# Rows of second chunks scaled between the halves of the value copy, first chunks' squares behind the next row copy, and a wait of its own for third chunks' last tile

## What is computed

```python
e = stack([tbl_f[ids[:, f]] for f in range(26)], axis=1)          # 512 x 26 x 64
x = layer_norm(dense @ Wd.T, gd, bd)                              # 512 x 128
y = layer_norm(einsum('bnd,ed->bne', e, Ws), gs, bs)              # 512 x 26 x 128
y = layer_norm(einsum('bne,pn->bep', y, Wsi), gsi, bsi)           # 512 x 128 x 32
T = concatenate([x[:, None, :], swapaxes(y, 1, 2)], axis=1)       # 512 x 33 x 128
Z = einsum('bnd,bmd->bnm', T, T)                                  # pair products
z = layer_norm(Z[:, TRIL_I, TRIL_J] @ Wl.T, gl, bl) * mask        # 512 x 512, 384 live
h = relu(concat([z, dense]) @ W_top1 + b1); h = relu(h @ W_top2 + b2)
out = h @ W_top3                                                  # 512 x 1
```

## Time and profile before

| what | us |
|---|---|
| median of three runs | 169.57 |
| time of the profiled execution | 170.27 |
| its span, first to last instruction | 168.4 |
| around the span | 1.87 |
| TensorE, VectorE, ScalarE, GpSimd busy | 147.9, 125.5, 82.7, 100.7 |

### The profile page before, as it was taken

The page is one execution under the profiler, slowest core; times in us unless marked ns, Lnnn a source line. Parts: engine busy times, 40 slices in busy tenths (PEclk is TensorE's granted clock), DMA queues, the critical chain, the costliest instruction groups (busy, mean ns, idle before and its releaser), DMA issues.

```text
span 168.4 us, 3523 instructions
## 1 busy us (share of the span) xinstructions
PE 147.9 (88%) x1378; PEld 106.1 (63%) x1378; DVE 125.5 (74%) x258; ACT 82.7 (49%) x226; POOL 100.7 (60%) x109
## 2 busy tenths in 40 slices
PE   0298978989799589999999899999998999889995
PEld 0133446957456457557978465778876665679983
...
DMA packets 5728, 8.14 MB, mean 48 GB/s; under 512 B 2357, under 2 KB 3279, under 8 KB 5712
## 3 DMA queue, kind: packets, MB, share of 16 engines
...
...
## 4 chain that ended last, share of the span: by engine, by line
POOL 49%; issue 24%; PE 17%; DMA 3%; ACT 2%; POOLq 1%; DVE 1%; SPq 1%; DVEq 0%
POOL G L333 49%; DMA smask<-in_span_mask_dram 3%; PE ps_y L1003 2%; PE ps_tail L1034 2%; PE ps_ut L1218 2%; PE ps_y L1202 1%; PE ps_tail L1161 1%; PE ps_z L1007 1%; POOLq L95 1%; PE ps_z L1034 1%; PE ps_z L1181 1%; PE ps_y L1092 1%; PE ps_gq L1060 1%; PE ps_z L1202 1%; PE ps_gq L1202 1%
## 5 line engine op out<-in xcount | busy, mean ns | idle before, releaser
L333 POOL DMA_INDIRECT G<-in_table_dram,idx x104 | 98.6, 948 | 34.6 <-issue 31.1
L1072 PE MATMUL ps_ut<-S,G 128*128 128x192 f32 (+4 forms) x128 | 21.9, 316 | 2.3 <-DVE G L775 2.3
L1072 PEld LDWEIGHTS ps_ut<-S,G 128*128 128x128 f32 x128 | 20.1, 199 | 4.0 <-DVE G L775 2.6
L789 DVE TENSOR_TENSOR V<-ps_y,bias_y 128x512 f32<-128x512 f32 x32 | 20.5, 683 | 1.3 <-PE ps_y L1085 1.2
L1092 PEld LDWEIGHTS ps_z<-V 128*64 128x64 f32 x448 | 14.3, 136 | 11.3 <-DVE V L805 6.5
L796 DVE TENSOR_REDUCE var<-sq 128x32 f32<-128x1024 f32 x14 | 17.1, 1221 | 5.6 <-ACT sq L439 5.6
L439 ACT ACTIVATE sq<-V 128x1024 f32<-128x1024 f32 x14 | 14.9, 1063 | 11.7 <-DVE V L789 11.5
L1085 PE MATMUL ps_y<-ut,wcg 64*128 64x512 f32 x64 | 18.1, 639 | 2.6 <-issue 1.5
L1092 PE MATMUL ps_z<-V 128*64 128x67 f32 x448 | 16.2, 224 | 0.8 <-DVE V L805 0.7
L1060 PE MATMUL ps_gq<-gram,gt 128*128 128x128 f32 x104 | 15.5, 289 | 1.6 <-ACT gt L425 1.4
L1060 PEld LDWEIGHTS ps_gq<-gram,gt 128*128 128x128 f32 x104 | 13.3, 198 | 2.8 <-ACT gt L425 1.7
...
## 6 DMA issues: line engine op xcount, KB each, us to landing
G<-in_table_dram,idx POOLq DMA_INDIRECT x104, 2.5
...
```

Source lines behind the costliest of these rows:

```text
L333: pool.indirect_dma_start(G[:, n // NC, j, g, :], None, table, bass.IndirectOffsetOnAxis(ap=idx[:, k:k + 1], axis=0)).then_inc(gathered[n ...
L789: dve.tensor_tensor(chunk_v(n)[:, g * CB // 2:(g + 1) * CB // 2, :, :], ps_y[:, g, :].rearrange("p (b l q) -> p b l q", l=2, q=NPROJ), bia ...
L1072: mm = pe.matmul(ps_ut[:, chunk % 2, col:col + width], G[:, gp, j, :, :].rearrange("p g d -> p (g d)"), S[:, j, :, :].rearrange("p s q -> ...
```

## The change

On VectorE, in slots c = 1 the rows of chunk n are scaled between the two halves of the value copy of chunk n - 1, and `variance2` of the first chunk leaves that slot; it stands in slot c = 2 after the two copies of `x_slots` and in front of `normalise2` (not in slot 2, where the chunk's variance is taken before the slots begin). On ScalarE, `square2` of the first chunk leaves slot c = 1 and stands in slot c = 2 behind `gt_copy`, with `ut_copy` behind it and `deviation2` after that; `relu2` goes in front of `deviation1`. On TensorE, the transposes of a third chunk begin after two tiles have arrived and wait for the third on a semaphore of its own; SyncE's load of the second part of wl waits for two tiles of chunk 2 instead of three. No instruction on data is added or removed.

```diff
--- before.py
+++ after.py
@@ -192,6 +192,7 @@
         ld_ids, ld_wc, ld_ws, ld_wd, ld_pm, ld_sm, ld_s, ld_x, ld_w1z, ld_w1d, ld_w2, ld_gs = [
             sem(n) for n in ("ld_ids", "ld_wc", "ld_ws", "ld_wd", "ld_pm", "ld_sm", "ld_s", "ld_x", "ld_w1z", "ld_w1d", "ld_w2", "ld_gs")]
         ld_wl = [sem("ld_wl_a"), sem("ld_wl_b")]
+        last_tile_gathered = [sem(f"last_tile_gathered{gp}") for gp in range(NG)]
         gathered = [[sem(f"gathered{gp}_{c}") for c in range(NC)] for gp in range(NG)]
 
         (idx_ready, consts_set, wc_ready, wcg_ready, wc_nat_ps, wc_nat_sb, gram_ps, gram_ready, patterns_ready, wsis_ready,
@@ -302,7 +303,7 @@
             sp.dma_start(pmask[:, :], pair_mask).then_inc(ld_pm, 16)
             sp.dma_start(mmask[:, :], merge_mask).then_inc(ld_pm, 16)
             for h, (k, end) in enumerate(((0, 2), (2, KB))):
-                sp.wait_ge(gathered[0][1 + h], 2 * len(batch(1 + h)) * 16)
+                sp.wait_ge(gathered[0][1 + h], 2 * (len(batch(1 + h)) - h) * 16)
                 sp.dma_start(wl[:, k:end, :], wl_blocks[:, k:end, :]).then_inc(ld_wl[h], 16)
             sp.wait_ge(gathered[0][3], 2 * len(batch(3)) * 16)
             sp.dma_start(w2s[:, :, :], w2).then_inc(ld_w2, 16)
@@ -332,7 +333,8 @@
                                 pool.wait_ge(done, value)
                         pool.indirect_dma_start(
                             G[:, n // NC, j, g, :], None, table,
-                            bass.IndirectOffsetOnAxis(ap=idx[:, k:k + 1], axis=0)).then_inc(gathered[n // NC][n % NC], 16)
+                            bass.IndirectOffsetOnAxis(ap=idx[:, k:k + 1], axis=0)).then_inc(
+                                last_tile_gathered[n // NC] if n % NC == 2 and j == js[-1] else gathered[n // NC][n % NC], 16)
 
             n = NCHUNK - 2
             pool.wait_ge(r2_ready, n + 1)
@@ -549,11 +551,15 @@
                     deviation3(gp - 1)
                 if not early:
                     gt_copy(n)
-                if c < 3:
+                if c < 2:
                     deviation2(n - 2)
+                if c == 2:
+                    square2(n - 2)
                 if c == 3 and gp > 0:
                     f_scale(gp - 1)
                 ut_copy(n - 1)
+                if c == 2:
+                    deviation2(n - 2)
                 if c == 0 and gp > 1:
                     relu1(gp - 2)
                 if c == 2 and gp > 0:
@@ -567,13 +573,14 @@
                 if n == 6:
                     prepare_gains((4,))
                     dense_direct(2)
-                deviation1(n)
                 if c == 1 and gp > 1:
                     relu2(gp - 2)
+                deviation1(n)
                 if c == 3 and gp > 0:
                     zn_copy(gp - 1)
-                square2(n - 1)
-                if c == 1:
+                if c != 1:
+                    square2(n - 1)
+                else:
                     z_evacuate(n - 2)
                 if c == 1 and gp > 1:
                     y_copy(gp - 2)
@@ -783,8 +790,8 @@
                     dve.tensor_copy(V[:, :, 1:3].rearrange("p (c i h) l -> p c i h l", h=2, c=NC)[:, :, :, h, :],
                                     x_sb[:, gp * GRAN:(gp + 1) * GRAN].rearrange("p (h l c i) -> p c i h l", h=2, l=2, c=NC)[:, :, :, h, :])
 
-            def y_evacuate(n):
-                for g in range(2):
+            def y_evacuate(n, halves=(0, 1)):
+                for g in halves:
                     dve.wait_ge(y_ps, 2 * n + 1 + g)
                     dve.tensor_tensor(chunk_v(n)[:, g * CB // 2:(g + 1) * CB // 2, :, :],
                                       ps_y[:, g, :].rearrange("p (b l q) -> p b l q", l=2, q=NPROJ),
@@ -917,17 +924,20 @@
                     z_merge(n - 3)
                 if c == 2 and gp > 0:
                     x_slots(gp)
+                    variance2(n - 2)
                 normalise2(n - 2)
                 if c == 3 and gp > 0:
                     root3(gp - 1)
                 if c == 0 and gp > 1:
                     add_dense(gp - 2)
                 variance1(n)
-                y_evacuate(n - 1)
+                y_evacuate(n - 1, (0, 1) if c != 1 else (0,))
                 scale_rows(n)
-                variance2(n - 1)
                 if c == 1:
+                    y_evacuate(n - 1, (1,))
                     z_merge(n - 2)
+                else:
+                    variance2(n - 1)
                 if n == 3:
                     prepare_shift()
 
@@ -1046,11 +1056,14 @@
 
             def transpose_rows(n):
                 gp, j, count = rows_of(n)
-                pe.wait_ge(gathered[gp][n % NC], 2 * count * 16)
+                split = n % NC == 2
+                pe.wait_ge(gathered[gp][n % NC], 2 * (count - split) * 16)
                 if n > 0:
 
                     pe.wait_ge(q_used, n)
                 for i in range(count):
+                    if split and i == count - 1:
+                        pe.wait_ge(last_tile_gathered[gp], 2 * 16)
                     mm = pe.transpose(ps_gq[:, i * P:(i + 1) * P], G[:, gp, j + i, :, :].rearrange("p g d -> p (g d)"), eye[:, :])
                 mm.then_inc(gt_ps, 1)
```

## The result

The changed kernel takes 173.79 us (median of 6 runs, 172.28 to 174.49), the kernel before 170.16 (median of 6 beside them, 169.30 to 171.87). The ratio is 1.0228, with a 95% interval of 1.0198 to 1.0259: slower, by a little more than 2% as far as the interval can tell. The prediction was 172.4 us, range 170.6 to 173.8, with 0.70 on a difference within 2% and 0.28 on slower by more. So the time lies just inside the range and the sign was right, but 3.6 us came where the sum gave 2.85, and the case on which most of the chance lay did not come.

What follows compares the result with a forecast made beforehand. TensorE's embed waiting for VectorE's first-chunk norm chain was taken as the bound, gathers a floor beneath. Delays of 1.45 + 0.70 + 0.70 = 2.85 us on 169.57 gave 172.4 us, range 170.6 to 173.8.

Steps and rivals of the forecast that it cites:

- the sum: Delays of embed in slots 6, 10 and 14 add 1.45 + 0.70 + 0.70 = 2.85 us to the time.
- the case on which most of the chance lay: Whole kernel: time differs by less than 2% (3.4 us) from the kernel before; chance 0.70.
- What bounds the kernel: Slots 6, 10, 14: embed starts 0.10 us after the first chunk's product, sharing its bank; gathers are a floor TensorE touches.
- The squares behind the row copy: Slots 6, 10, 14: squares to embed runs in series, 4.46 us; slot 6's embed comes 1.45 us later.
- The value copy's second half: Slots 10 and 14: split copy ends 2.09 us after its start instead of 1.28; embed 0.70 us later each.
- What these delays do afterwards: TensorE after embed: each delay is kept until the next slot c = 2 and reaches the end in full.
- What is saved: Earlier relu2 (0.74 us), VectorE's variance wait (0.43) and earlier row scaling (0.5) are counted at nothing.
- the lower end of 2.1: If the row copy held the squares, savings count: total 1.45 at slot 6, about 1.75 at 10, 2.1 us at 14.
- The gathers' own waits: GpSimd: gather 51 starts at 67.94, 0.2 us late, later ones lose some 0.3 more; hidden behind TensorE's lag.
- The last tile's own wait: Third chunks' transposes: separate wait worth zero, between -0.3 and +0.05 us; the earlier wl load also zero at the end.
- TensorE's clock falls in the new gaps: Rival, slots 6, 10, 14: lower clock costs 1.7 us three times, 5.1 in all, giving 177.5 us; chance 0.04.
- The rule that I set against the trace: Trainium skill on TensorE: waits inside a loop drop the clock again each time; would give the clock rival's 177.5 us.

Runs made afterwards that it cites:

- experiment 2: Changed kernel with first chunks' second-norm reciprocals in an SBUF tile and no wait of embed for the product: 172.09 us, ratio 1.0154.
- experiment 3: Kernel before with first chunks' second-norm reciprocals in an SBUF tile and no wait of embed for the product: 170.72 us, ratio 1.0062.
- experiment 10: Changed kernel with reciprocals of chunks 8 and 12 in PSUM bank ps_tail, embed of slots 10 and 14 not waiting: 171.11 us, ratio 1.0120.
- experiment 6: Changed kernel with old order of squares, variance, root and whole value copy; earlier relu2, last tile's wait, earlier wl load kept: 169.98 us, ratio 1.0003.
- experiment 5: Changed kernel with the value copy whole again and row scaling behind it, squares still behind the row copy: 172.11 us, ratio 1.0151.
- experiment 12: Changed kernel with six 128-column matmuls into an unused part of ps_y filling slot 6's gap alone: 173.32 us, ratio 1.0158.
- experiment 9: Changed kernel run again unaltered, for a second profile, against the kernel before: 173.43 us, ratio 1.0225.
- experiment 8: Kernel before with first chunks' reciprocals in SBUF, gathers' pacing waits removed, third chunks' last tile on its own semaphore: 171.40 us, ratio 1.0060.

## Why the prediction was off

*What bounds the kernel*: right. The bank wait in `embed` is real (0.10 us after the product in all six places; gone when the reciprocals move, experiments 2, 3 and 10), and the gathers are the floor under it (slot 14's last tile at 127.80 and 127.40 in experiments 3 and 6, however early TensorE came).

*The squares behind the row copy*: right. From the squares' entrance to `embed` 4.46 us were forecast; in slot 6 it is 68.82 - 64.40 = 4.42. The cost of slot 6 was forecast as 1.45 and is 1.41 (5.32 us from transposes to `embed` against 3.91).

*The value copy's second half*: right. 2.09 us were forecast from the copy's start to its end, and it is 97.88 + 0.68 - 96.39 = 2.17. Slots 10 and 14 were to cost 0.70 each and cost 0.76 and 0.79, in the second profile 0.69 and 0.77.

*What these delays do afterwards*: right, they are kept to the end (3.54 at slot 14, 3.6 in the span).

*What is saved*: half right. The wait for `relu2` went, but I counted nothing in its place; 0.38 us of waiting for the row scaling came (98.01 in the timeline above). Savings at nothing was the right choice: the lower end of 2.1 was not reached, since the second half of the copy and not the row copy decided in slots 10 and 14.

*The gathers' own waits*: gather 51 was forecast at 67.94 and had no wait, at 67.58, because slot 6 came sooner than before. In experiment 5, where slot 6 began at 64.45, it waited for the variance and started at 67.94. Later ones of the changed kernel waited 0.43, 0.85 and 0.93 us; all hidden, as forecast: no transposes waited behind slot 5.

*The last tile's own wait*, and wl: nothing at the end (experiment 6), right.

*TensorE's clock falls in the new gaps*: this is the step that failed. I gave it 0.04 and a price of 5.1 us, all three gaps or none, because one stretch had kept 1.00 with TensorE busy for 3.70 of 6.00 us. One stretch of one execution was taken as a rule, and it was not even like the new gaps: its idle time came in three pieces of 0.63, 1.02 and 0.53 us, where each new gap is one piece of 1.63 to 1.73, and 66 to 70 us is not busier, as I had said, but busy for 2.27 of 4.00. The sum so had no term for a fall in one gap of three. It is worth 1.49 us where it came (1.62 in experiment 12), and the clock of the whole span points to it in 5 of 11 executions; with it the profiled execution is accounted for: 1.41 - 0.91 + 1.49 + 0.76 + 0.79 = 3.54. Without it, in experiment 9, the delay at slot 14 is 2.22.

The rule that I set against the trace (TensorE: Matmul & The Clock Gate, HAM oscillation — how this bites in real kernels, of the Trainium skill) has the clock drop in every round of a loop with DMA waits of 3 to 5 us, a length that I had left out. No gap in front of `embed` is that long, so these runs do not test it; what they show is a fall once in an execution or not at all, where I had all three or none.

Two things stay open. The six executions with a clock of 0.97 or more have a median of 173.05, which is 3.5 above the 169.5 of the kernel before; the gaps explain 2.85 to 3.0 of it. Only one of those six has a profile (172.47 us, delays ending at +2.22). The two ways in which the start goes, with slot 6 up to 1.2 us apart, could make up the rest, but they can't be read from executions without a profile.

And what decides whether a given gap lets the clock fall was not found. Five profiles have such empty gaps of 1.63 to 1.73 us in front of `embed`, ten gaps in all (the changed kernel's two profiles and experiments 5, 10 and 12): the clock fell behind two of them, slot 6's of the first profile and slot 14's in experiment 12, and not in slot 6 of experiments 5, 9 and 10 with 1.72 and 1.73 us. At slot 5 it is otherwise: its transposes waited 0.86 us or more for a gather in eleven of the fourteen profiles, and in ten of these the clock of 54 to 58 us is below 1.00; with waits of 0.40 to 0.63 in the other three it is 1.00.

## What to carry to other kernels

Where small values lie in a bank that a later matmul writes, everything between them and that matmul is on TensorE's path: read the constant distance between a product's end and a matmul's start over several slots, and cost a reordering by it. A new idle gap of some 1.7 us on TensorE cost its own length and, in some executions, 1.5 to 1.6 us more of matmuls at the lower clock level; give it a term with a share of executions, not a yes or no, and take that share from more than one profile. The same goes for a remedy: one profile of a filled gap without a fall says nothing as long as the empty gap also has profiles without one. And before a PSUM operand of VectorE is moved to SBUF to free a bank, look at what GpSimd does beside it.

## What the runs showed of the chip

- One program, twice profiled, with equal gaps of 1.7 us: once a mean granted clock of 0.66 in the stretch of 4 us behind the first gap, once 1.00. Filling the gap of slot 6 with useless matmuls went with 1.00 there in two profiles of two, leaving it empty in three of four, so an effect of filling is not shown.
- A gather of 0.94 us that began inside a VectorE product of 1.22 us with both operands in SBUF ended no sooner than 0.81 us behind it and took up to 1.95 (15 gathers in four kernels); one that had begun before the product, or inside one with an operand in PSUM, kept its 0.94.
- With the wl load asked for two gathers earlier, slot 2's third tile was waited for 1.44 us, until 31.88; in experiment 8, where the load waits for all three tiles, they were transposed without a wait from 29.24 to 30.49. No effect at the end was seen (experiment 6).
